# Earlier loads of the shared experts' weights, rank products moved, and barriers without the GpSimd drain, in a two-layer attention and mixture-of-experts kernel

## The chip, the cores and the metric

The kernel runs on one core of one Trainium2 chip. The core has a matrix engine (TensorE, PE in the profile), a vector engine (VectorE, DVE), a scalar engine (ScalarE, ACT), GpSimd (POOL) and SyncE (SP), which here issues most of the DMAs and computes nothing. The metric is the device time of one execution in microseconds (us), as the median of the runs.

## The reference

Two layers, each an attention block and a feed-forward block with experts. Cut to what matters here:

```python
x = x + tanh(g_xattn[0]) * attention(layernorm(x), ctx, ctx)      # 4 x 512 tokens, width 512
x = x + tanh(g_ffn[0])   * ffn0(layernorm(x))                     # 8 experts, 2 per token
x = x + tanh(g_xattn[1]) * attention(layernorm(x), ctx, ctx)
x = x + tanh(g_ffn[1])   * ffn1(layernorm(x))                     # 32 experts, 6 per token
...
probs = softmax(x @ w_gate)            # ffn0; ffn1 takes sigmoid(x @ gate_w)
topk_w, topk_ids = top_k(probs, K)
routed = weighted sum over the chosen experts of (silu(x @ wg) * (x @ wu)) @ wd
shared = (silu(x @ sg) * (x @ su)) @ sd      # 1024 columns in ffn0, 384 in ffn1
return routed + shared
```

## The kernel before

The program is written by hand, engine by engine. Each of its four stages (attention 0, FFN 0, attention 1, FFN 1) is a block: every engine has its own list of instructions, semaphores order them, and at the block's end all engines meet at a barrier. At that end each engine first drains, GpSimd too. Between FFN 0 and attention 1 stands a further barrier of all engines (line 1885), at which GpSimd clears the semaphores that both layers use.

An FFN stage works on 2048 tokens, in four batches of 512 (B = 4), and runs like this:

- **Router.** DVE normalizes the tokens (`xh`), PE turns them, ACT copies them to `xT`, and PE forms the router's logits batch by batch (`logits_batch`, line 1056, and `turn_logits`, line 1065). Each batch of logits is copied by ACT and counted in `logits_in`. SP stores the four batches of `xh` to HBM (`xh_rows`, line 818, counted in `xh_stored`), since the experts gather tokens from there.
- **Choice of experts.** DVE computes the top experts of each token and a 0/1 matrix `mask` (counted in `mask_ready`), PE multiplies it with two constant matrices (`rank()`, line 1090, counted in `ranked`), and DVE works out each token's place in the table of the experts from that (lines 1523 to 1557). The table itself is built by PE from one-hot tiles that DVE (`tile_hot`, line 1630) and POOL (`slot_hot`, line 961) make.
- **Shared experts.** `shared_group(g)` handles batch g. Its products go over chunks of 128 columns (`shared_gu(g, f)`): eight chunks in FFN 0, three in FFN 1. A chunk is the gate product (o = 0) and the up product (o = 1), 16 matmuls of 512 columns in the trace for the first group, whose products take the raw weights (line 1116). The later groups take weights and tokens split into two parts (line 1120), which ACT and DVE prepare. Chunk n writes PSUM banks 0 and 1 or, for odd n, 2 and 3. In the first group ACT copies and activates a chunk's result (lines 1315, 1316), POOL multiplies (line 945) and splits it (line 934), and ACT and POOL split the down weights `w_sd_raw` (lines 1326, 940). Chunk n waits for POOL's product of chunk n - 2 (`h_made`). Then comes the down product (line 1150).
- **Routed experts.** Loops over tiles of 128 tokens: POOL gathers rows, PE multiplies (lines 1179, 1204), POOL scatters with addition (line 1000).

What the change touches lies at the start of an FFN and at the blocks' ends. SP's list at the start of an FFN is: the router's weights, a wait for POOL's constants (`ZEROED`), two stores of zeros, the stores of `xh` batches 0 and 1, then the shared experts' weights (FFN 0: the first four chunks, `load_raw`; FFN 1: `w_sh_gate` and `w_sh_up`), then the stores of `xh` batches 2 and 3, and, once all four stores have landed, `w_sd_raw`. In FFN 0 the further chunks are loaded by ACT. PE, after the last `turn_logits`, waits for all four batches of logits, then for the weights, does chunk 0, `rank()`, chunk 1 and so on. The wait for the logits stands there because `rank()` is in the stream behind it and because odd chunks write banks 2 and 3, which the router used.

## Time and profile before

| | us |
|---|---|
| median of 3 runs | 2057.18 (2054.80 to 2057.19) |
| the profiled execution's own time | 2056.58 |
| its span in the trace | 2054.9 |
| attention 0, attention 1 | 424.8, 423.9 |
| FFN 0, FFN 1 | 509.5, 693 |

The busy shares of the span are: PE 92%, DVE 66%, ACT 56%, POOL 38%; TensorE's granted clock is 0.966 of the full one on average. All starts are in us from the span's start. Attention 0 ends at 427.2, FFN 0 at 936.7, attention 1 at 1361.8. A line of a timeline gives the start, the duration, the engine and line, what is written from what, a count, and in brackets the idle time of the engine before it with what ended it. "SPq" and "POOLq" are the engines' sequencers, where DMA issues and semaphore instructions stand; "PEld" is PE's weight load.

### The profile page before, as it was taken

The page shows a single profiled execution, that of the slowest core. Times are in us where ns is not written, and L with a number is a line of the kernel's source. Part 1 is how long each engine was busy: PE and PEld are TensorE (multiplying, and loading weights), DVE is VectorE, ACT ScalarE, POOL GpSimd, SP SyncE. Part 2 cuts the span into 40 slices and gives each one's busy share as a digit, 9 for nine tenths or more (in the row PEclk, how much of TensorE's full clock was granted, in tenths as well). Part 3 has the DMA queues.
Part 4 walks back from the last instruction along what each step waited for, and adds up shares of the span by engine and source line. Part 5 has one row for each costly group of instructions (what it writes and reads, how often), then busy time and mean ns, then how long its engine had stood idle before and what let it go on. Part 6 is the DMA issues. An engine that isn't in the chain of part 4 may idle for free. (4 is left out here: it accounts for less than half of the span.)

```text
span 2054.9 us, 40817 instructions
## 1 busy us (share of the span) xinstructions
PE 1884.4 (92%) x10024; PEld 1220.0 (59%) x10025; DVE 1348.5 (66%) x2556; ACT 1144.9 (56%) x1856; POOL 783.2 (38%) x941
## 2 busy tenths in 40 slices
PE   4999999989999999993999999977888999999998
PEld 2333333344888877881433333344667888888886
DVE  6899988841445444434989898848995555555553
ACT  1777777743322335541677777762224666666664
POOL 3222222125301125553222222136653665565655
PEclk9999999989999999995899999988999999999998
DMA  4422222143111358765422222222026889899986
GB/s 139 119 59 65 59 66 69 35 146 120 52 52 62 134 171 197 144 110 138 120 61 67 62 61 63 52 87 87 1 73 178 197 188 207 201 201 203 199 197 107
DMA packets 100083, 233.53 MB, mean 114 GB/s; under 512 B 17410, under 2 KB 20484, under 8 KB 99972
## 3 DMA queue, kind: packets, MB, share of 16 engines
q1 hardware_dynamic: 61572, 137.75, 23.6%
q0 software_dynamic: 33792, 79.71, 20.1%
q10 hardware_dynamic: 4608, 14.68, 2.1%
q8 instruction: 58, 0.95, 0.2%
q14 instruction: 53, 0.43, 0.1%
HBM read 127.23 MB, written 57.67 MB: 90 GB/s over the span
## 5 line engine op out<-in xcount | busy, mean ns | idle before, releaser
L599 DVE TENSOR_REDUCE maxima<-ring_ps 128x1 f32<-128x512 f32 x1024 | 639.6, 680 | 89.3 <-PE ring_ps L386 88.5
L493 ACT ACTIVATE probs<-score_ps 128x1024 f32<-128x1024 f32 x512 | 501.7, 1018 | 91.6 <-PE score_ps L403 89.3
L386 PE MATMUL ring_ps<-k_turned,q_turned 64*128 64x512 f32 x1024 | 414.5, 482 | 39.3 <-DMA q_turned<-q_lo 18.4
L386 PEld LDWEIGHTS ring_ps<-k_turned,q_turned 64*128 64x128 f32 x1024 | 178.9, 193 | 366.7 <-DVE maxima L599 256.9
L1179 PE MATMUL bank_f<-w_gu_parts_f,xg_T_f 128*128 x1800 | 367.3, 352 | 2.6 <-issue 2.6
L1179 PEld LDWEIGHTS bank_f<-w_gu_parts_f,xg_T_f 128*128 128x128 f32 x1800 | 325.6, 190 | 30.8 <-issue 3.3
L403 PE MATMUL score_ps<-q_turned,k_turned 64*128 64x512 f32 x1024 | 336.7, 447 | 1.7 <-ACT probs L493 1.2
L420 PE MATMUL out_ps<-probs,v_ones 128*32 128x512 f32 x2048 | 273.3, 606 | 11.0 <-issue 10.3
L1204 PE MATMUL bank_f<-w_dn_parts_f,hg_T_f 96*128 (+1 forms) x888 | 242.9, 409 | 2.1 <-DVE hg_T_f L1771 1.5
L984 POOL DMA_INDIRECT xg_f<-xh_rows_f,idx_in_f x156 | 160.2, 1027 | 183.5 <-DVE idx_in_f L1661 116.8
L1000 POOL DMA_INDIRECT out_x<-y_tok_f,idx_out_f x111 | 176.8, 1593 | 131.5 <-ACT y_tok_f L1405 94.7
L1120 PE MATMUL bank_f<-x_parts_f,w_sh_parts_f 128*128 128x512 f32 x792 | 204.3, 394 | 0.0
L1204 PEld LDWEIGHTS bank_f<-w_dn_parts_f,hg_T_f 96*128 96x128 f32 (+1 forms) x888 | 157.3, 189 | 28.5 <-issue 3.3
L1120 PEld LDWEIGHTS bank_f<-x_parts_f,w_sh_parts_f 128*128 128x128 f32 x792 | 148.4, 190 | 26.9
L403 PEld LDWEIGHTS score_ps<-q_turned,k_turned 64*128 64x128 f32 x1024 | 146.1, 188 | 25.6 <-ACT probs L493 16.2
L961 POOL TENSOR_SCALAR slot_hot_f<-count_f_f,slot_of_f 128x128 fp32r<-128x128 f32 x128 | 97.1, 771 | 161.3 <-PE bank_f L1097 161.1
L1150 PE MATMUL bank_f<-w_sd_parts_f,h_parts_f 128*128 128x512 f32 x528 | 130.0, 406 | 17.0 <-DVE x_res L1726 8.3
L272 POOL CAST q_hi<-q_raw 128x512 fp32r<-128x512 f32 x30 | 18.4, 615 | 327.5 <-ACT q_raw L465 159.4
L1150 PEld LDWEIGHTS bank_f<-w_sd_parts_f,h_parts_f 128*128 128x128 f32 x528 | 102.3, 195 | 43.1 <-DVE x_res L1726 9.6
L289 POOL TENSOR_TENSOR scaled<-turned_out,recip 128x256 f32<-128x256 f32 x64 | 40.2, 628 | 212.0 <-DVE recip L607 212.0
L1670 DVE TENSOR_TENSOR w_gu_parts_f<-w_gu_f,w_gu_parts_f (+2 forms) x80 | 80.8, 1012 | 58.2 <-ACT w_gu_parts_f L1366 30.9
L1661 DVE CAST idx_in_f<-table_sb_f 128x1 int32 (+1 forms) x156 | 23.5, 152 | 141.9 <-issue 113.8
(231 smaller groups left out, 2343.4 us busy)
## 6 DMA issues: line engine op xcount, KB each, us to landing
w_gu_f<-in_L_w_gu SPq DMA_DIRECT2D x64, 384.0 KB
q_turned<-q_hi SPq DMA_DIRECT2D x128, 128.0 KB, 2.6
w_raw_f<-in_L_w_sh_gu ACTq DMA_DIRECT2D x28, 512.0 KB, 3.5
w_dn_f<-in_L_w_dn SPq DMA_DIRECT2D x32, 384.0 KB
k_turned<-k_hi SPq DMA_DIRECT2D x128, 64.0 KB, 2.1
q_turned<-no_max SPq DMA_DIRECT2D x64, 128.0 KB, 2.6
q_turned<-q_lo SPq DMA_DIRECT2D x64, 128.0 KB, 2.6
w_gu_f<-in_L_w_gu SPq DMA_DIRECT2D x16, 512.0 KB
```

The source lines that it names most:

```text
L386: pe.matmul(ring(k, "max", i), q_turned[rows, slot, h // 2, c * P:(c + 1) * P], k_turned[rows, slot, :], start=True, stop=True).then_inc(m ...
L403: mm = pe.matmul(score_ps[:, pair, a, :], k_turned[rows, slot, c * P:(c + 1) * P], q_turned[rows, slot, pair, :], start=True, stop=True)
L420: mm = pe.matmul(out_ps[32 * h:32 * h + 32, :], v_ones[:, u % RING, c, :], probs[:, (TPB * u + c) % PROBS, h // 2, h % 2, :], start=(c == ...
L493: act.activation(probs[:, (TPB * u + c) % PROBS, pair, :, :], score_ps[:, pair, :, :], ACT.Exp, scale=float(D) ** -0.5).then_inc(exped, 1)
L599: dve.tensor_reduce(maxima[:, par, col:col + 1], ring(k, "max", i), AX.X, ALU.max).then_inc(max_taken, 1)
L961: pool.tensor_scalar(slot_hot[:, n % HOTS, :], count_f[:], slot_of[:, i, k:k + 1], None, ALU.is_equal).then_inc(slot_hot_made, 1)
L984: pool.indirect_dma_start(xg[:, half, :], None, xh_rows, bass.IndirectOffsetOnAxis(ap=idx_in[:, half:half + 1], axis=0)).then_inc(gathered ...
L1000: pool.indirect_dma_start(acc_rows, bass.IndirectOffsetOnAxis(ap=idx_out[:, half:half + 1], axis=0), y_tok[:, half, :], None, compute_op=A ...
L1120: mm = pe.matmul(bank[:, 2 * (n % NBK) + o, :], w_sh_parts[:, o, w_part, d, :], x_parts[:, x_part, d, :], start=(d == 0 and j == 0), stop= ...
L1150: mm = pe.matmul(bank[:, 6 + c % 2, :], h_parts[:, h_part, f, c * P:(c + 1) * P], w_sd_parts[:, w_part, f, :], start=(f == 0 and j == 0), ...
L1179: mm = pe.matmul(bank[:, half, 0:2 * F], xg_T[:, half, x_part, d, :], w_gu_parts[:, bass.ds(par, 1), w_part, d, :].rearrange("p a f -> p ( ...
L1204: mm = pe.matmul(bank[:, 2 + half, :], hg_T[:, half, h_part, f, :], w_dn_parts[:, bass.ds(par, 1), w_part, f, :].rearrange("p a f -> p (a ...
```

## The change

Five edits:

1. In an FFN, SP issues the shared experts' weights right behind the router's weights, ahead of the wait for POOL's constants and of all stores.
2. PE's wait for the four batches of logits moves from before chunk 0 to before chunk 1.
3. `rank()` moves from behind chunk 0 to between the gate and the up product of chunk 1, in both layers.
4. In FFN 1, ACT runs a sigmoid on one column at its list's start, so that the table load stands there.
5. The attention and FFN blocks end without GpSimd's drain. The barrier between FFN 0 and attention 1 is one of four engines without GpSimd, ACT clears the semaphores, and GpSimd waits for a new semaphore `cleared`, which SP raises behind that barrier.

```diff
-        block = ctx.enter_context(nc.Block())
+        block = ctx.enter_context(nc.Block(no_gpsimd_drain=True))
...
             sp.dma_start(w_router[:, :, 0:E], t["w_router"].rearrange("(c p) e -> p c e", p=P)).then_inc(router_in, 16)
+
+            if layer == 0:
+                for n in range(RAWS):
+                    load_raw(sp, n)
+            else:
+                sp.dma_start(w_sh_gate[:], t["w_sh_gate"].rearrange("(c p) f -> p c f", p=P)).then_inc(weights_in, 16)
+                sp.dma_start(w_sh_up[:], t["w_sh_up"].rearrange("(c p) f -> p c f", p=P)).then_inc(weights_in, 16)
 
             sp.wait_ge(const_set, ZEROED)
...
-                if b == 1:
-
-                    if layer == 0:
-                        for n in range(RAWS):
-                            load_raw(sp, n)
-                    else:
-                        sp.dma_start(w_sh_gate[:], t["w_sh_gate"].rearrange("(c p) f -> p c f", p=P)).then_inc(weights_in, 16)
-                        sp.dma_start(w_sh_up[:], t["w_sh_up"].rearrange("(c p) f -> p c f", p=P)).then_inc(weights_in, 16)
...
-            pe.wait_ge(logits_in, B)
-
             if layer == 1:
                 pe.wait_ge(weights_in, 32)
...
+                if n == 1:
+
+                    pe.wait_ge(logits_in, B)
                 for o in range(2):
+                    if n == 1 and o == 1:
+                        rank()
...
                     shared_gu(g, f)
-                    if g == 0 and f == 0:
-                        rank()
...
+            if layer == 1:
+                act.activation(prob[:, 0, 0:1], gate[:, 0:1], ACT.Sigmoid)
             copy_batch(0)
...
+        cleared = ctx.enter_context(nc.semaphore("cleared"))
...
-        nc.all_engine_barrier(sems_to_clear=range(min(numbers), max(numbers) + 1))
+        nc.multi_engine_barrier([e.engine for e in (nc.sync, nc.scalar, nc.vector, nc.tensor)], sems_to_clear=range(min(numbers), max(numbers) + 1))
+        nc.sync.nop().then_inc(cleared, 1)
+        nc.gpsimd.wait_ge(cleared, 1)
```

SP at the start of FFN 1, before (FFN 0 has four loads of `w_raw` in the place of the two weight loads):

```order
L809 DMA w_router_f<-in_L_ffn_gate_w 128x4x32
L812 DMA xh_rows_f<-zero_tile_f 128x2x512 [waits ffn_const_set]
L814 DMA out_x<-zero_tile_f 128x2x512
L818 DMA xh_rows_f<-xh_f 128x4x512 [waits ffn_ln_done] x2
L826 DMA w_sh_gate_f<-in_L_ffn_sg 128x4x384
L827 DMA w_sh_up_f<-in_L_ffn_su 128x4x384
L818 DMA xh_rows_f<-xh_third_f 128x4x512 [waits ffn_ln_done]
L818 DMA xh_rows_f<-xh_fourth_f 128x4x512 [waits ffn_ln_done]
```

The same place of SP, after:

```order
L809 DMA w_router_f<-in_L_ffn_gate_w 128x4x32
L815 DMA w_sh_gate_f<-in_L_ffn_sg 128x4x384
L816 DMA w_sh_up_f<-in_L_ffn_su 128x4x384
L819 DMA xh_rows_f<-zero_tile_f 128x2x512 [waits ffn_const_set]
L821 DMA out_x<-zero_tile_f 128x2x512
L825 DMA xh_rows_f<-xh_f 128x4x512 [waits ffn_ln_done] x2
L825 DMA xh_rows_f<-xh_third_f 128x4x512 [waits ffn_ln_done]
L825 DMA xh_rows_f<-xh_fourth_f 128x4x512 [waits ffn_ln_done]
```

The two weight loads pass one wait for POOL and four DMAs.

PE at the end of the router in FFN 1, before; line 1065 is the last `turn_logits`, line 1116 a chunk, line 1090 `rank()`:

```order
L1065 MATMUL bank_f<-fold,logits_T_f 128x32 x3
L1116 MATMUL bank_f<-xT_f,w_sh_gate_f 128x512 [waits ffn_weights_in,ffn_logits_in]
L1116 MATMUL bank_f<-xT_f,w_sh_gate_f 128x512 x3
...
L1090 MATMUL bank_f<-mask_f,tri_f 128x512 [waits ffn_const_set,ffn_mask_ready]
L1090 MATMUL bank_f<-mask_f,ones_m_f 128x512
L1116 MATMUL bank_f<-xT_f,w_sh_gate_f 128x512 x4
```

The same place of PE, after:

```order
L1064 MATMUL bank_f<-fold,logits_T_f 128x32 x3
L1118 MATMUL bank_f<-xT_f,w_sh_gate_f 128x512 [waits ffn_weights_in]
L1118 MATMUL bank_f<-xT_f,w_sh_gate_f 128x512 x3
...
L1118 MATMUL bank_f<-xT_f,w_sh_gate_f 128x512 [waits ffn_logits_in]
L1118 MATMUL bank_f<-xT_f,w_sh_gate_f 128x512 x3
L1087 MATMUL bank_f<-mask_f,tri_f 128x512 [waits ffn_const_set,ffn_mask_ready]
L1087 MATMUL bank_f<-mask_f,ones_m_f 128x512
```

The two rank products stand one gate product later in PE's list, and the wait for the logits stands at chunk 1.

## Rows read from the trace of the kernel before

**Rows 1.** Busy by stage: PE, PEld, DVE, ACT, POOL, then PEclk, DMA share, GB/s; FFN 0, attention 1.
```profile
427.20:936.70 509.50, 485.25 (x2160) 377.85 (x2160) 214.84 (x457) 194.82 (x372) 168.57 (x163) 0.97 0.46 121
...
937.90:1361.80 423.90, 381.74 (x2272) 151.90 (x2272) 357.91 (x633) 297.85 (x374) 109.56 (x206) 0.93 0.29 74
```

**Rows 2.** Timeline of PE at the start of FFN 0.
```profile
446.00 1.80 PE L1065 MATMUL bank_f<-fold,logits_T_f 128*128 128x8 f32 x8 [0.72 <-ACT logits_T_f L1264]
450.83 9.84 PE L1116 MATMUL bank_f<-xT_f,w_raw_f 128*128 128x512 f32 x16 [3.03 <-DMA w_raw_f<-in_L_w_sh_gu]
460.50 0.38 PE L1090 MATMUL bank_f<-mask_f,tri_f 128*128 128x128 f32 x2
...
460.95 13.90 PE L1116 MATMUL bank_f<-xT_f,w_raw_f 128*128 128x512 f32 x32
476.46 1.98 PE L1116 MATMUL bank_f<-xT_f,w_raw_f 128*128 128x512 f32 x4 [1.62 <-POOL silu_T_f L945]
```

**Rows 3.** Timeline of ACT and POOL, 470 to 477 us.
```profile
471.98 0.63 ACT L1326 ACTIVATE w_sd_parts_f<-w_sd_raw_f 128x512 fp32r<-128x512 f32 x1 [8.70 <-DMA w_sd_raw_f<-in_L_ffn_w_sh_down]
...
475.14 1.27 POOL L945 TENSOR_TENSOR silu_T_f<-silu_T_f,y_tok_f 128x512 f32<-128x512 f32 x1
```

**Rows 4.** Timeline of SP's queue at the start of FFN 0.
```profile
441.66 5.20 SPq L798 DMA_DIRECT2D w_raw_f<-in_L_w_sh_gu  x4
...
460.78 0.37 SPq L832 DMA_DIRECT2D w_sd_raw_f<-in_L_ffn_w_sh_down  x1
```

**Rows 5.** Waits, engine and line waited for: us in total, times, longest.
```profile
DVE x_parts_f L1645 <- ACT x_parts_f L1291: 46.3, 1, 46.3
```

**Rows 6.** Instructions by line, ns min/median/max, first and last start: FFN ends, the clearing barrier.
```profile
L886 SPq EVENT_SEMAPHORE  x2: 17/17/17, 933.4 to 2054.3; - x2
...
L659 POOLq DRAIN  x2: 4449/6326/8202, 928.4 to 2050.2; - x2
...
L1885 POOLq EVENT_SEMAPHORE_RANGE_CLEAR  x1: 679/679/679, 937.1 to 937.1; - x1
```

**Rows 7.** Timeline of SP at the start of attention 1.
```profile
937.93 1.77 SPq L157 DMA_DIRECT2D x_res<-acc_rows_f  x4
```

**Rows 8.** Instructions of line 57, the attention blocks' ends.
```profile
L57 POOLq DRAIN  x2: 823/826/828, 426.1 to 1360.5; - x2
...
L57 DVEq DRAIN  x2: 17/20/24, 427.1 to 1361.6; - x2
```

**Rows 9.** Timeline of PE in FFN 1.
```profile
1380.65 1.30 PE L1065 MATMUL bank_f<-fold,logits_T_f 128*128 128x32 f32 x8 [0.72 <-ACT logits_T_f L1264]
1389.98 6.17 PE L1116 MATMUL bank_f<-xT_f,w_sh_gate_f 128*128 128x512 f32 x8 [8.03 <-DMA w_sh_up_f<-in_L_ffn_su]
...
1399.42 1.02 PE L1090 MATMUL bank_f<-mask_f,tri_f 128*128 128x512 f32 x2
...
1440.52 0.66 PE L1097 MATMUL bank_f<-tile_hot_f,slot_hot_f 128*128 128x384 f32 x1 [4.97 <-DVE tile_hot_f L1630]
```

**Rows 10.** Busy in a stretch of FFN 1, columns as in the first group.
```profile
1390.00:1395.00 5.00, 5.00 (x6) 2.12 (x7) 3.54 (x8) 0.00 (x0) 0.00 (x0) 0.50 0.71 277
```

**Rows 11.** Timeline of ACT and DVE in FFN 1.
```profile
1363.66 0.60 ACT L1256 ACTIVATE xT_f<-bank_f 128x512 f32<-128x512 f32 x1 [4.31 <-PE bank_f L1045]
...
1382.29 1.28 ACT L1286 ACT_TABLE_LOAD   x1
...
1391.39 0.69 DVE L1514 TENSOR_TENSOR mask_f<-above_f,tied_f 128x512 f32<-128x512 f32 x1
...
1401.40 0.69 DVE L1523 COPY total_t_f<-bank_f 128x512 f32<-128x512 f32 x1 [7.66 <-PE bank_f L1090]
...
1403.39 1.57 DVE L1527 TENSOR_TENSOR total_t_f<-cum_t_f,total_t_f 128x512 f32<-128x512 f32 x1
...
1406.06 1.31 DVE L1531 TENSOR_SCALAR cnt_i_f<-cum_t_f 128x32 int32<-128x32 f32 x1
1407.39 0.18 DVE L1532 TENSOR_SCALAR cnt_i_f<-cnt_i_f 128x32 int32<-128x32 int32 x1
```

More of the change, by code:

```diff
@@ L801, in make_ffn @@
         ZEROED, CONSTS = 13, 23
-        block = ctx.enter_context(nc.Block())
+        block = ctx.enter_context(nc.Block(no_gpsimd_drain=True))
         @block.sync
```

## The prediction

> **What bounds the kernel now.** I read the busy time by stage first, then the timelines around the four places that the change touches, then the waits. In FFN 0 PE is busy for 485 of 509.5 us [rows 1], so whatever moves PE's list there moves the stage's end. At its start PE idles twice: 3.03 us for the shared experts' weights, and 1.62 us before the fourth chunk, for POOL's product [rows 2]. The second goes back to a DMA as well: ACT stood 8.70 us waiting for `w_sd_raw`, so that POOL's product came only at 475.14 [rows 3], and SP, waiting for the last store of `xh`, could issue that load only at 460.78 [rows 4]. At FFN 0's end SP has seen the last scatter land at 933.4, but POOL's drain, which began at 928.4, takes 8.2 us, until 936.6 [rows 6]. The clear and the two barriers fill the rest until 937.93, when attention 1 issues its first load [rows 7]. At the start of FFN 1 PE idles 8.03 us for `w_sh_up`, and DVE, whose mask was ready at 1392.08, sits 7.66 us until the rank products are there [rows 9, 11]. From there DVE's chain is what counts: PE stands again at 1440.52, for DVE's one-hot tiles, for 4.97 us [rows 9]. So in FFN 1 a gain goes by when DVE gets the ranks, not by when PE starts.
>
> **FFN 0, start.** The router's last products end at 447.80 (446.00 + 1.80), and the weights will have landed: issued at about 428 instead of 441.66, with ten us before the first store of `xh` is due. Four issues took 5.20 us on SP between full queues [rows 4]; at the start SP has nothing else until POOL's constants come, so I cost the queue at nothing. PE thus starts chunk 0 3.03 us earlier. The chunk took 9.67 us to the rank products (450.83 to 460.50) [rows 2], part of it at the lower clock; I keep that. The rank products then stand 8 matmuls later, about 3.4 us at the 0.43 us that a matmul of this shape takes at the higher clock (32 in 13.90 us [rows 2]). So the ranks come at the same time as before, within 0.5 us. That costs nothing here, since DVE waits 46.3 us later on, for ACT and thus for PE [rows 5]. The 1.62 us: without the weights' 2 MB in between, the stores land earlier. The queues moved 7.3 MB from 438.5 to 460.7; at that rate 2.1 MB are 6 us. `w_sd_raw` is issued at about 455 and lands at about 466, after 11.2 us as now, POOL's product follows some 4.4 us later (471.98 to 475.14 plus 1.27) at about 470.5, and the fourth chunk is due at 471.7. The margin is one us, so I count the 1.62 us as gone, and 0 to 1.62 as its range. **Sum: 4.65 us** (3.0 to 4.9), hidden by nothing, as PE is the bound until the stage ends.
>
> **FFN 0, end.** SP's wait is over at 933.4, and from POOL's drain to attention 1's first load there are 1.33 us (936.6 to 937.93), the clear's 0.68 us among them [rows 6, 7]. No row shows that clear on ACT; I take the same 0.68 us, and 0 to 1.4 as bounds. The first load is then issued at 934.8: **3.1 us** (2.4 to 3.8). GpSimd waits for `cleared`, and behind that wait stand its memsets and, last, the first root, which DVE needs; at worst they start at 936.6 if POOL is really busy until then, 1.3 us earlier than now, which would cost 0.4 us of the 3.1.
>
> **Attention's ends.** POOL's drain of 0.83 us begins at 426.1, and is over at 426.9; DVE's own drain stands at 427.1 [rows 8]. DVE comes last, so removing POOL's is worth **0** (0 to 0.2), twice. At the program's end SP's wait is over at 2054.3 and the drain at 2050.2 + 4.45 = 2054.65 [rows 6]: **0.3 us**.
>
> **FFN 1, start.** Chunk 0 begins at 1381.95 (1380.65 + 1.30) instead of 1389.98. [...] The rank products come one gate product later, 8 x 0.43 = 3.43 us. So DVE has the ranks 8.03 - 3.43 = 4.6 us earlier, at 1396.8. The mask is due at 1390.8, 1.28 us earlier than now by the table load that leaves its path [rows 11], or at 1392.1 without that: either way before PE asks, at 1394.4. Edit 4 is therefore worth nothing; its price is hidden too: the load takes 1.28 us from about 1361.8, the one-column sigmoid 0.2, and ACT's first copy is due at 1363.66 [rows 11], 0.4 us later. POOL's products shift against DVE's chain. Now L1527 takes 1.57 us where the same shape alone takes 0.69 (L1514), and L1531 1.31 where L1532 takes 0.18 [rows 11]: 2.0 us lost while POOL was working. POOL's first three instructions will be largely done before DVE starts, so I take half of it back, 1.0 us. **Sum: 5.6 us.**
>
> **A rule on this.** What the rows show is that DVE's instructions stretch by 0.9 to 1.1 us where POOL works beside them. The Trainium skill's page "SBUF — State Buffer", section "Who interferes with whom", gives the mechanism: DVE instructions with two SBUF inputs, and some copies, share a port pair with GpSimd, and whichever is issued first keeps it for its whole instruction. By it a shift of either engine can win or lose one instruction's length each time; it names no sign, and is a rival below.
>
> The skill's page "ScalarE: Activation LUTs", section "What ACT_TABLE_LOAD costs", gives about 2.66 us for a switch of tables, the load's 1.28 us plus a drain. By that the first copy of `xT` would come 1 us late and the sum would lose up to 1 us. The trace shows 1.28 us with the next activation right behind it, and I go by that.
>
> **The sum.** 4.65 + 3.1 + 5.6 + 0.3 = 13.65 us off the profiled execution's 2056.58 (span 2054.9 and 1.7 around it): 2042.9. That execution is 0.6 us under the median and within the runs shown, so I correct nothing.
>
> **The rivals.**
> - *POOL is still waited for.* The blocks' barriers still count GpSimd. If its arrival stands behind the descriptor work that the drain showed, the 3.1 and 0.3 us stay: 2046.3. For it: the drain outlasts the landing by 3.2 us, so something in POOL is busy. Against it: at the program's end it is over 0.35 us after the landing. Chance 0.12.
> - *DVE's chain in FFN 1 meets POOL more often.* By the exclusive port, four of POOL's 1.27 us instructions [rows 3] that now miss the chain could hit it: 5.1 us more, FFN 1 gives 0.5 less 1.0, and the total is 4.65 + 3.1 + 0.3 - 0.5 = 7.5: 2049.0. For it: POOL has nine such instructions there, three per chunk. Against it: most of them collide already. Chance 0.10. The other way round, all of the 2.0 us and a short low stretch of the clock give 2.0 more: 2040.5, chance 0.08.
> - *The weights aren't there in time,* because they queue behind something the order doesn't show. Then PE starts where it did, the ranks come 3.43 us later, and FFN 0 gives nothing: 3.4 - 3.4 = 0, 2056.6. Chance 0.04.
> - *Slower: attention 1 stays longer at the low clock.* Its mean granted clock is 0.93 [rows 1], so of its 424 us some 59 run at 1.2 GHz (0.07 / 0.5 x 424): the level to which the clock fell while PE idled at the barrier. The change moves that start. PE is busy for 382 of the 424 us, and a matmul takes twice as long at 1.2 GHz, so each us more at that level costs up to 0.5 us. 27 us more eat the 13.65; twice the present stretch, 59 us more, gives 2042.9 + 29.5 = 2072.4. Against it: attention 0, which begins after no barrier of this kind, took 424.8 us, within 1 us of the same. Chance 0.03.
>
> **How the numbers follow.** The forecast has the rest, 0.63, with its own range of 2041.0 to 2045.0 from the bounds above. Down to 2039.5 and up to 2049.5 leave out only the last two rivals and tails, less than 0.15. About 0.2% (4.1 us) is what a measurement of this kernel can tell from no change; the first four cases are all beyond it: faster 0.92, same 0.05, slower 0.03.
>
> **What would show it.** In the profile after: PE's first line-1118 group follows the last line-1064 group with no wait for a DMA in either layer; no wait of PE for POOL before the fourth chunk of FFN 0; SP's attention 1 load 1.4 us behind the last scatter's landing; DVE's idle time before line 1525 in FFN 1 near 4 us instead of 7.66; and PE's wait for one-hot tiles grown from 4.97 to some 7 us, as PE gains 8 and DVE 5.6. FFN 0 about 4.7 us shorter, attention 1 the same length, FFN 1 about 5.9 shorter. I would be wrong if the drain's time turns up as a wait elsewhere, if FFN 0 keeps the 1.62 us, or if DVE's chain from the ranks to the first one-hot tile (24 us) comes out longer than before.

## The result, and the profile after

| | time, us | against before, same call |
|---|---|---|
| changed kernel, as first timed | 2045.42 (2041.4 to 2046.07, 4 runs) | 0.9939 [0.9926, 0.9953] |
| the same, second time | 2044.53 (2043.44 to 2049.86, 6 runs) | 0.9941 [0.9929, 0.9954] |
| the same, third time | 2044.07 (2042.3 to 2049.48, 6 runs) | 0.9941 [0.9926, 0.9955] |
| before, in the first of these calls | 2056.57 (2054.8 to 2057.19, 4 runs) | |

The change makes the kernel faster by 0.6%, 12.1 to 12.5 us by the ratios. The forecast was 13.65 us and 2042.9; the range held the time. Its sum got there partly by terms that were off in both directions, so part of the agreement is luck: in this first profile the start of FFN 0 gave 2.3 us more than forecast, the start of FFN 1 2.2 us less, and FFN 1's experts, for which nothing was forecast, took 4.2 us longer.

I cut both executions at the same seven points: SP's load of the router's weights (the FFN's start), PE's first gate and up product of an expert, and attention's first load. The two spans are 2054.9 and 2044.0.

| stretch, us | before | changed | gain |
|---|---|---|---|
| attention 0, up to the router's weights | 427.65 | 427.34 | 0.3 |
| FFN 0, from there to the first expert | 313.00 | 306.10 | 6.9 |
| FFN 0's experts and its exit | 197.28 | 192.71 | 4.6 |
| attention 1 | 423.93 | 423.97 | 0.0 |
| FFN 1, to the first expert | 193.09 | 189.71 | 3.4 |
| FFN 1's experts to the end | 499.95 | 504.17 | -4.2 |

The last line is where no edit reaches, apart from the 0.3 us at the program's end. It is taken up in the first experiment.

**FFN 0, start.** PE's timeline, as in [rows 2]; its columns are start, duration, engine and line, what is written from what, count, and the idle time before with what ended it:

```profile
445.70 1.06 PE L1064 MATMUL bank_f<-fold,logits_T_f 128*128 128x8 f32 x8 [0.72 <-ACT logits_T_f L1264]
446.61 10.55 PE L1118 MATMUL bank_f<-xT_f,w_raw_f 128*128 128x512 f32 x24
457.00 0.39 PE L1087 MATMUL bank_f<-mask_f,tri_f 128*128 128x128 f32 x2
...
469.30 31.17 PE L1118 MATMUL bank_f<-xT_f,w_raw_f 128*128 128x512 f32 x72 [1.40 <-POOL silu_T_f L944]
```

The 3.03 us for the weights are gone. What was not in the sum: 24 matmuls take 10.55 us here, 0.44 us each, while before 16 took 9.84. The router's last products, 1.06 us here and 1.80 before, show that the clock had not fallen, and the granted clock was 1.00 from 446.6 to 457.0. The wait for POOL ahead of the fourth chunk stayed, 1.40 us instead of 1.62. ACT and POOL, as in [rows 3], and SP, as in [rows 4]:

```profile
464.82 0.63 ACT L1328 ACTIVATE w_sd_parts_f<-w_sd_raw_f 128x512 fp32r<-128x512 f32 x1 [8.33 <-DMA w_sd_raw_f<-in_L_ffn_w_sh_down]
...
467.99 1.26 POOL L944 TENSOR_TENSOR silu_T_f<-silu_T_f,y_tok_f 128x512 f32<-128x512 f32 x1
...
427.77 1.92 SPq L798 DMA_DIRECT2D w_raw_f<-in_L_w_sh_gu  x4
...
453.99 0.37 SPq L831 DMA_DIRECT2D w_sd_raw_f<-in_L_ffn_w_sh_down  x1
```

POOL's product comes 7.15 us earlier than before (467.99 against 475.14), as the loads do. But PE comes as much earlier too, so it still stands there in this profile.

**FFN 0, end.** SP's wait for the last scatter, the clear, now on ACT, and the first load, as in [rows 6, 7]; the groups by line give ns min/median/max and first and last start:

```profile
L885 SPq EVENT_SEMAPHORE  x2: 17/17/17, 924.7 to 2043.6; - x2
...
L1888 ACTq EVENT_SEMAPHORE_RANGE_CLEAR  x1: 557/557/557, 925.4 to 925.4; - x1
```
```profile
926.15 1.77 SPq L157 DMA_DIRECT2D x_res<-acc_rows_f  x4
926.30 0.11 POOL L211 MEMSET minus_half<- 128x16 f32 x1 [4.60 <-SPq L1889]
```

From the landing to the first load it is 1.45 us instead of 4.53: 3.1 us, as forecast. The clear takes 0.56 us on ACT, where the forecast had 0.68. GpSimd is free 0.15 us behind SP. The time of its drain shows up nowhere.

**FFN 1, start.** PE and DVE, as in [rows 9, 11]:

```profile
1368.93 1.27 PE L1064 MATMUL bank_f<-fold,logits_T_f 128*128 128x32 f32 x8 [0.72 <-ACT logits_T_f L1264]
1370.01 5.19 PE L1118 MATMUL bank_f<-xT_f,w_sh_gate_f 128*128 128x512 f32 x8
...
1381.91 1.02 PE L1087 MATMUL bank_f<-mask_f,tri_f 128*128 128x512 f32 x2
...
1409.92 0.71 PE L1122 MATMUL bank_f<-x_parts_f,w_sh_parts_f 128*128 128x512 f32 x2 [1.55 <-DVE w_sh_parts_f L1652]
1413.14 0.41 PE L1094 MATMUL bank_f<-tile_hot_f,slot_hot_f 128*128 128x384 f32 x1 [2.51 <-DVE tile_hot_f L1632]
...
1424.14 0.54 PE L1094 MATMUL bank_f<-tile_hot_f,slot_hot_f 128*128 128x384 f32 x1 [2.56 <-DVE tile_hot_f L1632]
```
```profile
1383.90 0.69 DVE L1525 COPY total_t_f<-bank_f 128x512 f32<-128x512 f32 x1 [3.56 <-PE bank_f L1087]
1384.62 1.83 DVE L1527 TENSOR_TENSOR_SCAN cum_t_f<-reset_t_f,total_t_f 128x512 f32<-128x512 f32 x1
1386.49 1.57 DVE L1529 TENSOR_TENSOR total_t_f<-cum_t_f,total_t_f 128x512 f32<-128x512 f32 x1
...
1391.00 1.19 DVE L1535 TENSOR_SCALAR tiles_f_f<-cnt_i_f 128x32 f32<-128x32 int32 x1
...
1397.88 1.21 DVE L1547 CAST slot_of_f<-part_i_f 128x96 f32<-128x96 int32 x1
...
1408.02 1.76 DVE L1652 TENSOR_TENSOR w_sh_parts_f<-w_sh_gate_f,w_sh_parts_f 128x512 fp32r<-128x512 f32 x1
...
1411.38 4.98 DVE L1632 SCALAR_TENSOR_TENSOR tile_hot_f<-count_f_f,tile_of_f,entry_f 128x384 fp32r<-128x384 f32 x5
```

The 8.03 us are gone. DVE has the ranks 33.8 us after the FFN's start (1350.12) instead of 39.5 (1401.40 - 1361.86): 5.8 us earlier. But its chain from there to the first one-hot tile takes 27.5 us (1411.38 - 1383.90), where before it took 24.1. Five instructions lose 5.1 us: lines 1534 and 1535 take 1.19 us each on 32 columns, and 0.18 before [rows 11]; the cast on line 1547 takes 1.21, and 0.21 before; line 1652 takes 1.76 twice, and 0.68 and 0.78 before. The scan on line 1527 loses 0.6 more (1.22 before), and other lines give 2.4 back, 1.0 of them the second 128x1536 product (1.81 us, and 2.81 before), so that 3.4 remain. Most of these come back, though. Line 1652 and the first two tiles meet four additions of POOL's on line 965, which fell on later lines of DVE's before: on its sixth and seventh tile and on the two wide products behind them. DVE in the changed kernel and before, and POOL in the changed kernel:

```profile
1417.46 1.75 DVE L1554 TENSOR_TENSOR chosen_f<-row_f,top_rows_f 128x1536 f32<-128x1536 f32 x1
...
1423.38 2.21 DVE L1632 SCALAR_TENSOR_TENSOR tile_hot_f<-count_f_f,tile_of_f,entry_f 128x384 fp32r<-128x384 f32 x4
```
```profile
1431.81 2.84 DVE L1552 TENSOR_TENSOR chosen_f<-row_f,top_rows_f 128x1536 f32<-128x1536 f32 x1
...
1439.74 2.56 DVE L1630 SCALAR_TENSOR_TENSOR tile_hot_f<-count_f_f,tile_of_f,entry_f 128x384 fp32r<-128x384 f32 x4
```
```profile
1406.16 4.75 POOL L965 TENSOR_TENSOR x_res<-x_res,y_tok_f 128x512 f32<-128x512 f32 x2
```

The last line of each DVE fence begins with the eighth tile. From the ranks to there it is 39.5 us (1423.38 - 1383.90) and was 38.3 (1439.74 - 1401.40), so 1.1 of the 3.4 us are lost and the rest is only moved. What PE waits for has changed too: before, it stood once for the one-hot tiles, 4.97 us; here it stands 1.55 us for line 1652 and 2.51, 0.68 and 2.56 us for one-hot tiles, 7.3 in all, with some 7 forecast.

### The profile page after: what moved, and what is told of

Its sections match the earlier page's. It is cut to its first block and busy times, and to the rows that moved or that the text cites. A ratio compares the mean times of both kernels' runs of the same rounds, so it can differ in the third digit from the quotient of the medians.

```text
span 2044.0 us, 40829 instructions
## 1 busy us (share of the span) xinstructions
PE 1886.2 (92%) x10024; PEld 1220.2 (60%) x10025; DVE 1348.0 (66%) x2556; ACT 1145.5 (56%) x1857; POOL 782.2 (38%) x941
## 5 line engine op out<-in xcount | busy, mean ns | idle before, releaser
L1179 PEld LDWEIGHTS bank_f<-w_gu_parts_f,xg_T_f 128*128 128x128 f32 x1800 | 325.8, 190 | 30.4 <-issue 3.0
L1663 DVE CAST idx_in_f<-table_sb_f 128x1 int32 (+1 forms) x156 | 23.5, 152 | 147.8 <-issue 118.6
```

Source lines behind the costliest of these rows:

```text
L1179: mm = pe.matmul(bank[:, half, 0:2 * F], xg_T[:, half, x_part, d, :], w_gu_parts[:, bass.ds(par, 1), w_part, d, :].rearrange("p a f -> p ( ...
```

## The experiments

All versions but two start from the changed kernel or from its variant with the ranks behind chunk 0. The stage lengths of all profiles stand together here, in us: start of the FFN to the first expert, then the rest of the FFN; "ranks" is when DVE reads them in FFN 1, "chain" from there to the first one-hot tile.

| version | FFN 0 | rest | ranks | chain | FFN 1 | rest | ratio to before |
|---|---|---|---|---|---|---|---|
| before | 313.0 | 197.3 | 39.5 | 24.1 | 193.1 | 500.0 | |
| before, again | 312.8 | 196.5 | 38.6 | 24.1 | 192.0 | 503.3 | |
| barriers alone | 314.5 | 192.5 | 39.5 | 24.1 | 193.6 | 503.2 | 0.9988 [0.9979, 0.9996] |
| weights alone | 307.8 | 196.2 | 32.0 | 23.3 | 184.6 | 502.9 | 0.9947 [0.9935, 0.9960] |
| changed | 306.1 | 192.7 | 33.8 | 27.5 | 189.7 | 504.2 | 0.9939 |
| changed, second | 307.4 | 195.4 | 31.9 | 27.5 | 186.0 | 502.1 | 0.9941 |
| changed, third | 309.5 | 192.9 | 31.9 | 27.5 | 186.0 | 503.6 | 0.9941 |
| no sigmoid ahead | 307.9 | 194.9 | 33.8 | 27.5 | 189.8 | 501.6 | 0.9945 [0.9926, 0.9964] |
| narrow products | 306.4 | 196.2 | 31.9 | 19.3 | 181.1 | 502.9 | 0.9906 [0.9889, 0.9924] |
| ranks behind chunk 0 | 306.8 | 193.8 | 30.9 | 23.8 | 184.2 | 503.6 | 0.9921 [0.9909, 0.9934] |
| the same in FFN 1 alone | 306.2 | 193.4 | 31.6 | 24.1 | 185.1 | 500.5 | 0.9919 [0.9906, 0.9932] |
| and the wait moved | 306.3 | 192.3 | 30.4 | 23.5 | 184.3 | 502.8 | 0.9919 [0.9906, 0.9931] |
| split in the gaps | 306.6 | 194.1 | 31.1 | 22.8 | 183.6 | 502.4 | 0.9909 [0.9892, 0.9926] |
| all three | 306.3 | 196.3 | 30.3 | 22.8 | 181.7 | 500.7 | 0.9904 [0.9889, 0.9919] |

### Is the expert stage's loss real?

Theory: the 4.2 us in FFN 1's experts vary from run to run. Rival: they belong to the change. The changed kernel unchanged, and the kernel before unchanged:

> The changed kernel once more, for its time with more rounds and for a second profile. Theory A, the 4.2 us that the routed experts of FFN 1 took longer in the first profile are not from the change but vary from run to run: the stretch from the first line-1167 product of FFN 1 to the end comes out at least 1.5 us away from the first profile's 505.8 us, and runs of the kernel spread over more than 3 us again. Rival B, they belong to the change (POOL and DVE meet at another phase): 505.8 within 1 us.

> The kernel before once more, for a second profile of it. Theory A: the first profile's 504.5 us for FFN 1 from its first line-1167 product to the end was a short draw, as four profiles of other versions with the same expert code show 506.6 to 508.7 us; this one shows 506 to 509. Rival B, the expert stage of the kernel before is really some 3 us shorter than that of the versions: 504 to 505 us.

The rest of FFN 1 took 502.1 and 503.6 us in two more profiles of the changed kernel, 503.3 in the second of before, and 500.5 to 503.6 in the other versions; no edit of any of them reaches there. The first profile of before had a short one (500.0) and the first of the changed kernel a long one (504.2); two versions with most of the change's edits had 500.5 and 500.7, and two with one edit alone 502.9 and 503.2. The means are 501.6 us for before (two profiles) and 503.3 for the changed kernel (three); profiles of the changed kernel alone differ by 2.1. So the 4.2 us can't be put down to the change, and whether it has a small part in them isn't shown. In the expectations I had cut that stage 3 to 5 us earlier, at the first turn of gathered rows, where the order of two neighbouring tiles blurs the cut; with the cut at the first expert's product the second profile is 2.1 us off the first. The loss is spread thinly: between the 40th and the 60th tile PE, ACT and POOL wait for each other a few tenths of a us at a time. Why the phase falls one way or the other isn't shown.

### The barriers alone

```
-        block = ctx.enter_context(nc.Block())
+        block = ctx.enter_context(nc.Block(no_gpsimd_drain=True))
...
-        nc.all_engine_barrier(sems_to_clear=range(min(numbers), max(numbers) + 1))
+        nc.multi_engine_barrier([e.engine for e in (nc.sync, nc.scalar, nc.vector, nc.tensor)], sems_to_clear=range(min(numbers), max(numbers) + 1))
+        nc.sync.nop().then_inc(cleared, 1)
+        nc.gpsimd.wait_ge(cleared, 1)
```

> The kernel before with the barrier part alone (blocks without GpSimd's drain, the clear between the layers without GpSimd, and GpSimd's wait for `cleared`). Theory A, each part acts in its own place: SP's first load of attention 1 comes 1.2 to 1.6 us after the last scatter's landing instead of 4.5 us, the program's end gains 0.3 us, and all else keeps its length: 2056.6 - 3.1 - 0.3 = 2053.2 us. Rival B, GpSimd is really busy until its drain's end and the time comes back as a wait behind the barrier: within 0.5 us of 2056.6.

Measured: 2054.76 us, 2.5 us off by the ratio (0.8 to 4.3 by its interval), with 3.4 expected. SP ends its block and issues attention 1's load 1.3 us later, where the second profile of before has 4.4:

```profile
L659 SPq DRAIN  x2: 7/7/7, 932.3 to 2054.4; - x2
```
```profile
933.63 1.77 SPq L157 DMA_DIRECT2D x_res<-acc_rows_f  x4
933.78 0.11 POOL L211 MEMSET minus_half<- 128x16 f32 x1 [4.96 <-SPq L1887]
```

Rival B, within 0.5 us of before, lies just outside the interval, and GpSimd starts attention 1's work 0.15 us behind SP. Attention 1 took 424.3 us.

### The weights alone

```
+            if layer == 0:
+                for n in range(RAWS):
+                    load_raw(sp, n)
+            else:
...
             sp.wait_ge(const_set, ZEROED)
```

> The kernel before with the early weight loads alone; the rank products still stand behind chunk 0 and the wait for the logits before it. Theory A, the early weights carry FFN 0 and the rank move is what FFN 1 could do without: FFN 0 starts 6 to 7 us earlier, of which 3.0 is the wait for the weights and the rest is chunk 0 running at 2.4 GHz; in FFN 1 the ranks reach DVE 3.4 us earlier than in the changed kernel (30.4 us after the stage's start instead of 33.8), so the shared stage ends 3.4 + 3.4 us earlier than before: 2056.6 - 6.7 - 6.8 = 2043.1. Rival B, the wait for the logits (about 0.5 us of idle PE before chunk 0) keeps the granted clock at 0.50 through chunk 0: FFN 0 gives 3.0 us, chunk 0 of FFN 1 takes 13 us instead of 8.8, and the total is 2056.6 - 3 - 3 = 2050.6.

Measured: 2046.48 us, 10.9 us off before by the ratio (8.2 to 13.4 by its interval). One part of five brings most of the gain, and the ranks come as early as in the changed kernel's best profile, at 32.0 us, with the chain at 23.3 us. PE in FFN 1:

```profile
1375.67 5.40 PE L1115 MATMUL bank_f<-xT_f,w_sh_gate_f 128*128 128x512 f32 x8 [0.37 <-ACT logits_f L1267]
...
1385.49 1.12 PE L1089 MATMUL bank_f<-mask_f,tri_f 128*128 128x512 f32 x2 [0.99 <-DVE mask_f L1513]
```

PE waits 0.37 us for the logits and then 0.99 us for the mask. Theory A had the mechanism, and its sizes only roughly: FFN 0 gave 5.1 us instead of 6.7 (312.9, the mean of before, against 307.8), FFN 1 8.0 instead of 6.8 (192.6 against 184.6). The profile thus shows 13.1 us where the timed ratio has 10.9, and theory A's 2043.1 lies below all five timed runs (from 2044.78). Rival B's clock is there at chunk 0's start, 5.40 us for a gate product that takes 3.68 at 2.4 GHz, but B's 2050.6 is far off.

### The ranks' place

The changed kernel with the ranks back behind chunk 0, and the wait for the logits back ahead of it:

```
+            pe.wait_ge(logits_in, B)
...
-                if n == 1:
-                    pe.wait_ge(logits_in, B)
...
-                    if n == 1 and o == 1:
-                        rank()
...
+                    if g == 0 and f == 0:
+                        rank()
```

> The changed kernel with one part undone: the rank products stand behind chunk 0 and the wait for the logits ahead of it, as before. Theory A: DVE gets FFN 1's ranks up to 3.4 us earlier than in the changed kernel (it can take them when `weight` is done, 30.3 us after the stage's start), which is worth 2 to 3.4 us: 2045.4 - 2.7 = 2042.7. Rival B: PE's idle time for the logits keeps its clock low through chunk 0 in one or both layers, 2 to 4 us lost: 2048.4. Rival C: within 1 us of 2045.4, as the order of the ranks doesn't matter.

The ranks back in FFN 1 alone (`if layer == 0 and n == 1 and o == 1` and `if layer == 1 and g == 0 and f == 0`), with the wait for the logits left where the change has it, beside a third timing of the changed kernel:

> The changed kernel with the rank products of FFN 1 alone back behind chunk 0 (FFN 0 as changed, and no wait for the logits ahead of chunk 0 in either). Theory A, the rank move costs its 3 us in FFN 1 alone: ranks 28.5 to 29 us after the stage's start, DVE's chain from there to the first one-hot tile 24 us instead of 27.5, first one-hot tile at 54 to 55 us instead of 59.4 to 61.3, the shared stage 180 to 182 us, and the time is that of the version with both moved back, 2041.6 within 1.5 us. Rival B, the cost lies in FFN 0: 2044 to 2045.

> The changed kernel on this chip beside the others, for its time and a third profile. Expected 2044.5 to 2045.4 us; chain from the ranks to the first one-hot tile in FFN 1 27.5 us again by theory A (GpSimd's products always fall on the same DVE instructions); a chain that differs by over 1 us would speak for chance meetings.

Measured: 2041.61 and 2038.98 us, ratios 0.9921 and 0.9919, against 0.9941 for the changed kernel timed beside each; 2.9 and 5.1 us by the medians. The intervals overlap by their ends, but the direction is the same twice and the profiles say where: in FFN 1 alone. The ranks come 0.3 to 3 us earlier, the chain is 24 us instead of the 27.5 of all three profiles of the changed kernel, and the stage up to the first expert is 184 to 185 us instead of 186 to 190. So **the move of the ranks costs time**: 3 to 5 us by the medians, 1 to 5.5 by the stage. The second version's expectation had the chain right and the rest not: its ranks came at 31.6 us instead of 28.5 to 29, since chunk 0's gate product took 6.01 us at the lower clock, the stage was 185.1 us instead of 180 to 182, and its time lies below the range, with a short expert stage (500.5). POOL's lines 944, 939 and 933 show the other side. In the changed kernel they hold DVE up; with the ranks behind chunk 0 POOL is held up more often itself:

```profile
1388.42 1.28 POOL L944 TENSOR_TENSOR silu_T_f<-silu_T_f,y_tok_f 128x512 f32<-128x512 f32 x1 [0.91 <-ACT silu_T_f L1318]
1389.66 1.27 POOL L933 TENSOR_TENSOR h_parts_f<-silu_T_f,h_parts_f 128x512 fp32r<-128x512 f32 x1
1390.89 1.26 POOL L939 TENSOR_TENSOR w_sd_parts_f<-w_sd_raw_f,w_sd_parts_f 128x512 fp32r<-128x512 f32 x1
```
```profile
1394.79 0.21 DVE L1546 CAST slot_of_f<-part_i_f 128x96 f32<-128x96 int32 x1
...
1397.56 2.79 POOL L944 TENSOR_TENSOR silu_T_f<-silu_T_f,y_tok_f 128x512 f32<-128x512 f32 x1 [2.87 <-ACT silu_T_f L1317]
```

The first fence is the changed kernel, beside DVE's lines 1534 and 1535 at 1389.78 and 1391.00: each begins just behind a product of POOL's and ends with it. The second is the version with both moved back: the same cast takes 0.21 us, and POOL's product 2.79 instead of 1.28, behind DVE's wide product at 1397.46. Of the 3.7 us between the two chains (23.8 and 27.5), 2.1 lie in line 1652, which meets POOL's line 965 in the changed kernel alone; that part is moved and not lost, as in FFN 1's start above. From the ranks to the eighth tile it is 38.1 us with both moved back, 38.3 in FFN 1 alone and 39.4 to 39.5 in the changed kernel. With the later ranks, the eighth tile comes 1.3 to 4.4 us later in the changed kernel (71.3 to 73.3 us after the stage's start against 69.0 and 70.0).

### GpSimd's products narrowed

The cause itself: the changed kernel with POOL's nine products of FFN 1's first group on 2 of 512 columns, so the lower parts of h and of `w_sh_down` are left out there (two memsets of POOL's set them to zero beforehand).

```
+            W = S if layer == 0 else 2
...
-                pool.tensor_tensor(out=w_sd_parts[:, 1, f, :], in0=w_sd_raw[:, f, :], ...
+                pool.tensor_tensor(out=w_sd_parts[:, 1, f, 0:W], in0=w_sd_raw[:, f, 0:W], ...
```

> The changed kernel with GpSimd's nine products of the first group in FFN 1 (three each of silu times up, the lower parts of h and of w_sh_down) on 2 of 512 columns, and the lower parts set to zero beforehand, so that work is left out in this place alone. Theory A, DVE's chain in FFN 1 is stretched by these products: from line 1525's start to the first one-hot tile it takes 27.5 us in two profiles of the changed kernel, and 6.0 us fewer here (21.5), as lines 1527 to 1547 fall back to the times that they show where GpSimd is idle (0.69 for 128x512, 0.2 for 128x96); the shared stage, in which DVE is busy for 95% of the time, ends 4 to 6 us earlier, and the kernel takes 2040. Rival B, the chain's length is DVE's own: 27 us within 1 us and the time unchanged.

Measured: the chain takes 19.3 us, 8.2 fewer (6.0 expected), the stage 4.9 us fewer at equal ranks (181.1 against 186.0), and the time is 2039.74, 4.3 us under the least of the changed kernel's three medians. DVE's lines in it, the counterparts of 1529, 1535 and 1547, and one product of POOL's:

```profile
1388.19 0.69 DVE L1535 TENSOR_TENSOR total_t_f<-cum_t_f,total_t_f 128x512 f32<-128x512 f32 x1
...
1390.41 0.18 DVE L1541 TENSOR_SCALAR tiles_f_f<-cnt_i_f 128x32 f32<-128x32 int32 x1
...
1394.90 0.21 DVE L1553 CAST slot_of_f<-part_i_f 128x96 f32<-128x96 int32 x1
...
1397.57 1.76 DVE L1562 TENSOR_TENSOR chosen_f<-chosen_f,weight_f 128x1536 f32<-128x1536 f32 x1
...
1397.60 1.78 POOL L950 TENSOR_TENSOR silu_T_f<-silu_T_f,y_tok_f 128x2 f32<-128x2 f32 x1 [5.53 <-ACT silu_T_f L1324]
```

Both directions show: DVE's short lines are short again, and POOL's product on two columns, 0.20 us elsewhere in this profile, takes 1.78, until DVE's product that began 0.03 us before it ends. The Trainium skill's page "SBUF — State Buffer", section "Who interferes with whom", says that DVE instructions with two SBUF inputs, and casts and `tensor_scalar` in the modes with two ports, share a pair of ports with GpSimd, and that whichever is issued first keeps it for its whole instruction. The trace agrees on all three kinds (1.57 against 0.69, 1.21 against 0.21, 1.19 against 0.18). With 19.3 us as the chain's length without such meetings, the kernel before lost 4.8 us of its 24.1 to them. Of the 8.2 us, 2.1 are line 965 again (line 1652's two take 0.69 and 0.78 us here): from the ranks to the eighth tile it is 33.3 us, 6.1 fewer.

### The sigmoid ahead

```
-            if layer == 1:
-                act.activation(prob[:, 0, 0:1], gate[:, 0:1], ACT.Sigmoid)
```

> The changed kernel without the one-column Sigmoid. Theory A, in the changed kernel the table load has nowhere to show: the mask comes 1.3 us later but still 2 us before PE asks for it in the second chunk, so the time stays within 1 us of the changed kernel (2045), and DVE gets the ranks at the same time after the stage's start (31.9 to 33.8 us). Rival B: the later DVE chain ends after the rank products' time and FFN 1 loses 1.3 us.

Measured: 2046.98 us (2039.79 to 2052.16), ranks at 33.8, chain 27.5, stage 189.8, as in the changed kernel's first profile. The time alone, with runs 12 us apart, could not tell; the profile shows that in that place the sigmoid hides nothing. With the ranks behind chunk 0 it does: there PE's wait of 0.99 us for the mask is in the version without the sigmoid and not in the one with it (0.64 us of idle DVE ahead of line 1524 instead).

### The wait moved, the split in the gaps, and all together

From the version with the ranks behind chunk 0. First, PE's wait for the logits stands behind chunk 0 as well; its banks don't need it:

```
-            pe.wait_ge(logits_in, B)
...
                     if g == 0 and f == 0:
+                        pe.wait_ge(logits_in, B)
                         rank()
```

> The version with the ranks behind chunk 0 in both layers, with the wait for the logits moved from ahead of chunk 0 to ahead of the rank products. Theory A: chunk 0 begins 0.3 to 0.4 us earlier in each layer; FFN 0 keeps it (0.3 us), FFN 1 not, as the mask is due 0.1 us before or after PE asks; 2041.3, within 0.5 us of the version with the wait. Rival B, PE's short wait is what lets the clock fall ahead of chunk 0, and without it the chunk runs at 2.4 GHz from its start: 1.5 to 3 us less.

Second, FFN 1's first split of the shared weights goes where ACT and DVE stand idle:

```
+            first_w_hi(0)
             copy_logits(B - 2)
             copy_logits_T(B - 1)
+            first_w_hi(1)
             copy_logits(B - 1)
...
+                for o in range(2):
+                    dve.wait_ge(sw_hi, o + 1)
+                    dve.tensor_tensor(w_sh_parts[:, o, 1, :, :], raw_w(FC, o), ...
                 dve.wait_ge(activated, 1)
```

> The version with the ranks behind chunk 0, and FFN 1's first split of the shared experts' weights moved: ACT makes the two upper parts in its 1.2 us gaps between the copies of the logits, DVE the two lower parts before it waits for `prob`, where it is idle for 10 us. Theory A, DVE bounds FFN 1's shared stage, so the 0.68 + 0.77 us of line 1651 there leave its chain and the first one-hot tile comes 1.4 us earlier (22.4 instead of 23.8 us after line 1524's start), 2041.6 - 1.4 = 2040.2 us. Rival B, ACT's copies miss their gaps and push the logits, or POOL meets the chain at another phase: within 1 us of 2041.6 or above.

Third, all together, with FFN 0's split of `w_sh_down` one chunk later on ACT and POOL:

```
-                for part in range(2 * f, min(FC, 2 * f + 2)):
+                late = 1 if layer == 0 else 0
+                for part in range(max(0, 2 * (f - late)), min(FC, 2 * (f - late) + 2)):
```

> The version with the ranks behind chunk 0, the wait for the logits behind it too, FFN 1's first weight split in the gaps, and in FFN 0 the split of w_sh_down one chunk later on ACT and GpSimd, so that neither stands for w_sd_raw ahead of the second chunk's silu. Theory A: the gains add up, 2041.6 - 1.4 (split in the gaps) - 0.3 (wait) - 0 to 1.4 (GpSimd's product in time) = 2039.2 us, the fastest of all. Rival B: PE waits for nothing there in most runs (the version with the ranks behind chunk 0 showed no wait for GpSimd ahead of the fourth chunk of FFN 0), and it stays at the 2039.8 of the version with the split in the gaps.

Measured: 2039.87, 2039.84 and 2038.31 us. The last is the fastest of all, 0.9904 [0.9889, 0.9919], whose interval ends below that of the changed kernel on the same chip, 0.9941 [0.9926, 0.9955]; it is 5.8 us under it by the medians. PE in the first of the three, FFN 0 and FFN 1:

```profile
446.04 8.63 PE L1113 MATMUL bank_f<-xT_f,w_raw_f 128*128 128x512 f32 x16
...
1369.14 3.68 PE L1113 MATMUL bank_f<-xT_f,w_sh_gate_f 128*128 128x512 f32 x8
1372.66 3.60 PE L1113 MATMUL bank_f<-xT_f,w_sh_up_f 128*128 128x512 f32 x8
1377.89 1.10 PE L1087 MATMUL bank_f<-mask_f,tri_f 128*128 128x512 f32 x2 [1.64 <-issue]
```

In FFN 1 chunk 0 runs at 2.4 GHz throughout and PE then waits for the mask (DVE's line 1514 ends at 1377.79), so the ranks move by only 0.6 us. The time of this version, 2039.87, lies outside theory A's 2041.3 within 0.5, and in rival B's range. Whether the wait for the logits makes the clock fall isn't settled: chunk 0's gate product took 5.15 to 5.40 us in all three profiles that have that wait behind early weights, and without it 3.68 in five profiles and 5.19 to 6.01 in three. The wait is not needed for the fall, and one profile of each version can't show more.

And the last version, PE in FFN 0 and the split in DVE's idle time in FFN 1:

```profile
455.61 29.78 PE L1117 MATMUL bank_f<-xT_f,w_raw_f 128*128 128x512 f32 x69
...
1370.40 0.69 DVE L1513 TENSOR_TENSOR w_sh_parts_f<-w_sh_gate_f,w_sh_parts_f 128x512 fp32r<-128x512 f32 x1 [5.38 <-ACT w_sh_parts_f L1285]
```

PE runs 69 matmuls on end from the ranks on, past the fourth chunk, with no wait for POOL. That can't be put down to the later split: with the ranks behind chunk 0 alone PE ran 107 matmuls on end there as well, as rival B had it. The chain is 0.8 us shorter, not 1.4 (22.8 against 23.5): DVE meets POOL elsewhere, on the second 128x1536 product, 2.79 us instead of 1.76. Each of the small gains lies under what a measurement can tell; their sum against the changed kernel does not, and most of that sum is the ranks' place (2041.61 us, ratio 0.9921).

## Why the prediction was right, and where it was not

I compare means of three profiles of the changed kernel with those of the two of before.

- **FFN 0, start: forecast 4.65, measured 5.2 us** (312.9 against 306.1, 307.4 and 309.5). The 3.03 us for the weights went, as said. The 1.62 us went for the reason given in two profiles of three. In the first the wait stayed at 1.40 us and the clock gave the rest: PE began the fourth chunk 6.8 us earlier in the FFN, and POOL's product came as much earlier. In the second and third POOL's product ends 1.7 us and more before PE is due at the fourth chunk (467.76 + 1.26 against 470.7 in the second), since PE ran at the lower clock there, as the forecast had it. In the third profile the clock had fallen, and here is the same list at the lower clock:

```profile
447.28 1.88 PE L1064 MATMUL bank_f<-fold,logits_T_f 128*128 128x8 f32 x8 [0.72 <-ACT logits_T_f L1264]
449.01 13.00 PE L1118 MATMUL bank_f<-xT_f,w_raw_f 128*128 128x512 f32 x24
...
462.29 13.90 PE L1118 MATMUL bank_f<-xT_f,w_raw_f 128*128 128x512 f32 x32
```

  Chunk 0 and the gate product behind it take 13.00 us instead of 10.55, the granted clock was 0.50 from 449 to 454 us (1.2 GHz), and PE never stands for POOL. So the margin of one us between POOL's product and the fourth chunk was sized for the lower clock in chunk 0. The step that failed in the first profile is "part of it at the lower clock; I keep that": chunk 0's clock is no constant of the place. Chunk 0 and the gate product behind it took 10.55, 12.10 and 13.00 us, where the forecast had 13.1 (9.67 and 3.43).
- **FFN 0, end: forecast 3.1, measured 3.1** at the exit (1.45 us from landing to first load instead of 4.53), in every version with that part. The rest of FFN 0, exit included, took 3.2 us less on average (196.9 against 193.7), but it scatters: 196.2 us with the weights alone, and 192.3 to 196.3 in the versions with the shorter exit. The rival of a wait that stays fell.
- **Attention's ends: forecast 0, measured 0.2** (427.5 against 427.3; the weights alone, whose blocks end as before, show 427.1, so this is no gain that a profile can tell), and 0.3 at the program's end, from SP's last wait to the span's end: 0.4 (2043.6 to 2044.0) instead of 0.6 (2054.3 to 2054.9), 0.2 in these rows, which are given to a tenth.
- **FFN 1, start: forecast 5.6, measured 5.3 us** (192.6 against 189.7, 186.0 and 186.0), by two errors that cancel. Against the first profile of before, the ranks came not 4.6 but 5.8 us earlier, and 7.6 in two profiles (5.3 and 7.2 against the mean of both). The forecast took chunk 0 to be as long as before; its first eight matmuls took 6.17 us then, 5.19 in the first profile and 3.68 in the other two, where it did not run at the lower clock at all. And the chain did not get 1.0 us back, but grew by 3.4 to the first tile and by 1.1 to the eighth, so this term was 2.1 us off. That is the step that failed: "POOL's first three instructions will be largely done before DVE starts". POOL's first was, at 1381.32; the next two wait for ACT, and ACT for `w_sd_raw`, so they began at 1384.11, 0.2 us behind DVE's first line, and took 3.41 us. They start by a transfer, not by PE's list, and so the move of the chunk said nothing about them. The forecast also stopped at line 1532 of before: it took 2.0 us as lost to POOL, where the narrow products put 4.8 on the whole chain. Taken to the eighth tile, the term closes: the ranks came 6.5 us earlier by the means (39.1 and 32.5), the way from there is 1.1 us longer, and the stage gave 5.3. The rival of more meetings had the mechanism, and took 5.1 us for it; measured are 3.4 to the first tile and 1.1 to the eighth. What it left out is that the ranks gained more than it allowed. Its counterpart took all of the 2.0 us and a short low stretch of the clock; of that the clock's half came true beside it.
- **Edit 4 is worth nothing: right**, in the place where the change has the ranks. ACT's first copy of `xT` came 0.5 us behind the sigmoid's start, and no sooner was there work for it.
- **Slower by attention 1: did not occur.** It took 424.0, 424.4 and 424.4 us, before 423.9 and 424.5.
- **The sum.** 5.2 + 3.2 + 5.3 + 0.2 less 1.7 for FFN 1's experts (means 501.6 and 503.3, chance as far as is shown) is 12.2 us, by the ratios 12.1 to 12.5; forecast 13.65. That the total fits so well owes something to luck: FFN 1's two errors, 1.9 us too little for the ranks and 2.1 too much for the chain, cancel. Two of the three signs that the forecast named for being wrong did appear, the chain in every profile and the wait for POOL in one. Two slips in its arithmetic change nothing here: PE asks for the mask at 1394.8 and not 1394.4, and 2.0 us under 2042.9 are 2040.9 and not 2040.5. What I did not ask is whether each edit pays for itself: the weights alone are worth 10.9 us by the ratio, the barriers 2.5 (3.1 at the exit by the profiles), and the move of the ranks takes 3 to 5 back by the medians. These add up to 8.3 to 10.5 us and not to the 12.1 to 12.5 of the whole; the intervals leave room for that.

Open: why the clock falls in one execution at the router's last products and not in another; and why a first one-hot tile that comes 8.2 us earlier, with narrow products, makes the stage only 4.9 us shorter. For 2.1 us the traces show it: they are line 965's meetings, which come later with narrow products and so leave the eighth tile 6.1 us earlier and not 8.2 (65.2 and 71.3 us after the stage's start). PE, whose down product ends at 54.4 us there and at 55.0 in the changed kernel's second profile, can't use the first tile at 51.2 either. Up to the eighth tile it then stands 6.2 us for DVE (0.65 and 5.54) instead of 9.2 (2.92, 2.51 and 3.80). Where the other 1.2 us of the 6.1 go I have not followed.

## What to carry to other kernels

Before you move a product so that PE need not wait, ask when the engine behind it gets its result: the late rank products removed a wait of 0.4 to 1.4 us on PE and made the chain on DVE, which was the bound, 1.1 to 1.4 us longer to the eighth tile and its start up to 3 us later. Measure such a chain to a point behind the last meeting: to the first tile it seemed 3.4 us longer, and 2.2 of these were meetings that had only moved forward. Where DVE and GpSimd work side by side, price a shift by which of GpSimd's instructions start from something else (here a transfer) and will now fall on DVE's short ones: each cost DVE up to 1.1 us here, beside products of 1.27 us. And before a gap of some us between two profiles is explained, profile the same kernel again: stages that no edit touched differed by up to 4 us.

## What the runs showed of the hardware

- A DVE instruction of 0.18 us took 1.19 where it met one of GpSimd's, and one of GpSimd's on two columns took 1.78 us instead of 0.20 where it met one of DVE's (128x1536, two inputs).
- The granted clock at the same place of the same kernel differs from one execution to the next: the eight router products that end ahead of chunk 0 took 1.06 us in one and 1.88 in two others, and from 449 to 454 us of the third profile it was 0.50:

```profile
449.00:454.00 5.00, 5.00 (x7) 2.17 (x8) 3.82 (x26) 0.51 (x2) 0.00 (x0) 0.50 0.77 286
```

  (The columns are length, busy time of PE, PEld, DVE, ACT and POOL, granted clock, DMA share and GB/s.) Profiles of one kernel differed by up to 3.4 us at the start of FFN 0 (306.1 to 309.5), with the granted clock at 1.00 in the one and 0.50 in the other where chunk 0 begins.
- GpSimd's drain at a block's end outlasted the landing of its last scatter by 3.2 us [rows 6], and no wait turned up elsewhere when it was left out.
